# Attention and experts on one core: eight value products moved into the first five steps, the shared expert's preparation to the middle, the feed-forward weight splits to the end

## The reference, cut to what matters

```python
def _L0_attn_ref(X, Wq, bq, Wk, bk, Wv, bv, Wo, bo, gamma, beta, lam):   # B=2, S=1024, E=128, H=16, D=64
    Q = einsum('bse,hec->bhsc', X, Wq) + bq; K = einsum('bse,hec->bhsc', X, Wk) + bk    # c = 2D
    V = einsum('bse,hed->bhsd', X, Wv) + bv
    A1 = einsum('bhqd,bhkd->bhqk', Q[..., :d], K[..., :d]) / sqrt(d)
    A2 = einsum('bhqd,bhkd->bhqk', Q[..., d:], K[..., d:]) / sqrt(d)
    P = softmax(A1) - lam * softmax(A2)
    O = einsum('bhqk,bhkd->bhqd', P, V)
    Y = concat_heads(O) @ Wo + bo
    return layernorm(Y) * gamma + beta, times 0.2

def _L0_ffn_ref(x, alpha, w_gate, b_gate, W1m, b1m, W2m, b2m, W1e, b1e, W2e, b2e):
    main = gelu(x @ W1m + b1m) @ W2m + b2m                       # the shared expert, 128 -> 512 -> 128
    probs = softmax(mean(x, axis=1) @ w_gate + b_gate)           # 8 experts, top 2 of each batch
    expert_out = sum over the two of gate * (gelu(x @ W1e[k] + b1e[k]) @ W2e[k] + b2e[k])
    return a * main + (1 - a) * expert_out                       # a = clip(alpha, 0.1, 1)

xn = layernorm(x)
out = x + attn(xn) + ffn(xn)
```

## Time and profile before

| | |
|---|---|
| time, median of 3 runs (lowest to highest) | 1177.14 us (1176.85 to 1177.73) |
| the profiled execution's own time, and its span | 1176.92 us, 1175.1 us |
| PE, share of the span busy | 96% |
| POOL, ACT, DVE | 83%, 81%, 77% |

### The profile page before, as it was taken

How to read it: one execution, slowest core, us unless ns; L and a number is a source line. 1 busy time by engine, 2 the same in 40 slices (tenths; PEclk the granted TensorE clock), 3 DMA queues, 4 the chain that set the end, 5 groups by cost and what they waited for, 6 DMA issues and landing times.

```text
span 1175.1 us, 27816 instructions
## 1 busy us (share of the span) xinstructions
PE 1128.0 (96%) x9730; PEld 779.9 (66%) x9730; DVE 904.8 (77%) x1573; ACT 949.8 (81%) x1711; POOL 979.9 (83%) x609
## 2 busy tenths in 40 slices
PE   5899999999999999999999999999999999998998
PEld 4666666666666666666666666666666666664797
DVE  7878888888888888888888888888888888874510
ACT  3288899888898888898888898888898988885432
POOL 2589999999999999998888999999898888899000
PEclk9999999999999999999999999999999999998999
DMA  8942222222211222122212211222222212100000
GB/s 196 344 115 61 48 63 61 61 61 62 53 42 44 61 61 56 45 78 56 55 46 56 50 35 37 56 56 56 56 56 56 56 45 56 43 5 1 1 19 18
DMA packets 76439, 71.28 MB, mean 61 GB/s; under 512 B 43380, under 2 KB 65396, under 8 KB 76404
## 3 DMA queue, kind: packets, MB, share of 16 engines
q1 hardware_dynamic: 75396, 70.65, 23.1%
q10 hardware_dynamic: 880, 0.19, 0.1%
q0 software_dynamic: 128, 0.01, 0.0%
HBM read 22.59 MB, written 14.68 MB: 32 GB/s over the span
## 4 chain that ended last, share of the span: by engine, by line
PE 63%; ACT 20%; issue 6%; POOL 6%; DVE 4%; ACTq 1%; DMA 0%; DVEq 0%; SPq 0%; POOLq 0%
PE ps L567 20%; PE ps L535 18%; ACT work L753 11%; PE ps L553 10%; PE ps L489 8%; ACT p_mix L753 6%; POOL p_mix L448 3%; PE ps L652 3%; ACT pt L766 3%; PE ps L639 2%; POOL work L445 2%; PE ps L516 1%; DVE small L947 1%; DVE pt L903 1%; ACT small L719 0%
## 5 line engine op out<-in xcount | busy, mean ns | idle before, releaser
L947 DVE TENSOR_REDUCE small<-ps 128x1 f32<-128x1024 f32 x512 | 614.3, 1220 | 168.3 <-PE ps L535 168.3
L448 POOL TENSOR_TENSOR p_mix<-p_mix,work 128x1024 f32<-128x1024 f32 x256 | 608.8, 2378 | 21.4
L766 ACT ACTIVATE pt<-ps 128x512 f32<-128x512 f32 x512 | 306.8, 599 | 131.8 <-PE ps L553 129.7
L553 PE MATMUL ps<-ident,p_mix 64*128 64x64 f32 x4096 | 353.1, 227 | 5.6 <-POOL p_mix L448 2.8
L445 POOL TENSOR_SCALAR work<-work,small 128x1024 f32<-128x1024 f32 x256 | 307.4, 1201 | 50.4 <-DVE small L972 48.3
L553 PEld LDWEIGHTS ps<-ident,p_mix 64*128 64x128 f32 x4096 | 305.6, 139 | 55.9 <-issue 37.2
L753 ACT ACTIVATE p_mix<-ps,small 128x1024 f32<-128x1024 f32 x256 | 286.5, 1119 | 16.7 <-DVE small L947 16.7
L753 ACT ACTIVATE work<-ps,small 128x1024 f32<-128x1024 f32 x256 | 285.1, 1114 | 0.1
L567 PE MATMUL ps<-pt,v_h 128*64 128x512 f32 x1024 | 250.2, 610 | 0.7 <-ACT pt L766 0.7
L535 PE MATMUL ps<-k_hi,q_hi 64*128 64x512 f32 x512 | 227.5, 444 | 5.9 <-ACT p_mix L753 3.4
L535 PE MATMUL ps<-k_hi,q_lo 64*128 64x512 f32 x512 | 225.8, 441 | 0.0
(11 more groups left out here) (135 smaller groups left out, 1211.0 us busy)
## 6 DMA issues: line engine op xcount, KB each, us to landing
qx_hi<-q_hi SPq DMA_DIRECT2D x64, 256.0 KB, 3.8
qx_lo<-q_lo SPq DMA_DIRECT2D x64, 256.0 KB, 4.6
v_scratch<-pt SPq DMA_DIRECT2D x16, 512.0 KB, 5.4
v_h<-v_scratch SPq DMA_DIRECT2D x32, 256.0 KB, 3.1
w_scratch<-wqk_hi SPq DMA_DIRECT2D x16, 160.0 KB, 1.8
w_scratch<-wqk_lo SPq DMA_DIRECT2D x16, 160.0 KB, 1.9
wqk_hi<-w_scratch SPq DMA_DIRECT2D x16, 160.0 KB, 2.2
wqk_lo<-w_scratch SPq DMA_DIRECT2D x16, 160.0 KB, 2.3
```

What stands on the lines that cost most here:

```text
L448: pool.tensor_tensor(e1, e1, e2, ALU.add).then_inc(mix_done, 1)
L553: mm = pe.transpose(pt_ps[:, c * D:(c + 1) * D], p_mix[rows, col:col + P], ident[rows, rows])
L766: act.activation(pt4[:, kb % 2, :, j * P + half * D:j * P + (half + 1) * D], pt_ps.rearrange("p (c q) -> p c q", c=KC), ACT.Copy).then_inc ...
L947: dve.tensor_reduce(neg_max[:, m:m + 1], slot[SLOT[k, s]], AX.X, ALU.max, negate=True)\
```

## The change

**Values.** Parts 0 and 1 are computed before the second batch is transposed, parts 2 to 23 after it, and parts 24 to 31 inside steps 0 to 4 (two in each of the first three, one in each of the next two), behind the scores of the step. Parts 3, 7, 11, 15, 19 and 23 are copied out by ACT and get their bias from POOL, in SBUF. The other parts stay with DVE. SP stores tiles 0 to 11, then loads the values of head 0, then stores tiles 12 to 14, and tile 15 in its turn for head 1. POOL fills `y_acc` (`start_y`) after the weight split of head 1 in place of before it. In steps 0 to 7 the inverse sums come between the two row maxima.

**Experts.** The chosen experts' loads come after SP's work for head 2, and the preparation of the shared expert is spread over steps 119, 123, 127, 131, 135 and 139.

**First-layer weights.** The high parts are made by ACT, the low parts by DVE: one set after step 255, two after step 256 and two after step 257. The first hidden unit on PE comes one step earlier, and so does the first gelu on ACT.

```diff
-SET_MAIN = 5 + B
+SET_MAIN = 5 + 2 * B
+MAIN_AT, INPUT_AT = (119, 123), (127, 131, 135, 139)
...
+SPLIT_AT = {STEPS - 1: (0,), STEPS: (1, 2), STEPS + 1: (3, 4)}
+V_LATE = {0: (24, 25), 1: (26, 27), 2: (28, 29), 3: (30,), 4: (31,)}
+V_EARLY = 24
...
+        def by_act(u):
+            return u < V_EARLY and u % 4 == 3
+        def v_free(u):
+            return max([w for w in range(u) if v_place(w) == v_place(u)], default=None)
+        def v_out(u):
+            count = sum(by_act(w) == by_act(u) for w in range(u + 1))
+            return (v_copied if by_act(u) else v_evac), count
+        def v_place(u):
+            if u in (2, 3):
+                return u - 2
+            if u < V_EARLY + 2:
+                return 4 + (u + 2) % 4
+            return 6 if u in (26, 28) else 7
+        def v_part(u):
+            i, hv = divmod(u, 2)
+            return v_st[:, i % TB, hv * BANK:(hv + 1) * BANK]
...
-            for i in range(NT):
-                sp.wait_ge(v_evac, 2 * i + 2)
+            def store_v(i):
+                for u in (2 * i, 2 * i + 1):
+                    if by_act(u):
+                        sp.wait_ge(v_added, u // 4 + 1)
+                    else:
+                        sp.wait_ge(*v_out(u))
                 sp.dma_start(v_scratch[i, :, :], v_st[:, i % TB, :]).then_inc(v_stored[i % TB], 16)
+            for i in range(V_EARLY // 2):
+                store_v(i)
...
             for v in v_stored:
-                sp.wait_ge(v, 16 * B)
+                sp.wait_ge(v, 16)
             load_v(0, 0, 0)
+            for i in range(V_EARLY // 2, NT - 1):
+                store_v(i)
...
+                if n == 1:
+                    store_v(NT - 1)
...
+                if n == 2:
+                    load_experts()
+                if n == IT // B - 2:
+                    for v in v_stored:
+                        sp.wait_ge(v, 16 * B)
...
+                if n == MAIN_AT[1]:
+                    pool.tensor_scalar(w2[:, 0:HC * E], w2[:, 0:HC * E], coef[:, 0:1], one, ALU.mult, ALU.mult)\
+                        .then_inc(set_step, 1)
+                    pool.wait_ge(set_step, 3)
+                    pool.tensor_tensor(bias[:, 0, :], bias[:, 0, :], gb_bc[:, E:2 * E], ALU.add).then_inc(set_step, 1)
+                if n in INPUT_AT:
+                    part = INPUT_AT.index(n)
+                    pool.wait_ge(set_step, 5)
+                    add_row(bias[:, 0, :], part * TB // 2, (part + 1) * TB // 2)
...
-            start_y()
             for n in range(1, NW):
                 split_w(n)
-            set_main()
+            pool.wait_ge(xn_ready, 2 * B)
+            start_y()
+            def bias_v(first, end):
+                for u in range(first, end, 4):
+                    pool.wait_ge(*v_out(u))
+                    hv = u % 2
+                    pool.tensor_tensor(v_part(u), v_part(u), bv_bc[:, hv * BANK:(hv + 1) * BANK], ALU.add)\
+                        .then_inc(v_added, 1)
+            bias_v(3, V_EARLY)
...
-                s_ = k - TB - 1
-                if isinstance(g, int) and g == STEPS // BODY - 1 and 0 <= s_ < SETS:
-                    pool.wait_ge(s_ready, 2 * TB * (IT - 1))
-                    pool.tensor_scalar(w1_hi[s_], w1r3[:, s_, :], one, one, ALU.mult, ALU.mult)\
-                        .then_inc(w1_split, 1)
...
+            def values(u):
+                i, hv = divmod(u, 2)
+                if u in (2, 6):
+                    pe.wait_ge(lo_done, 1 if u == 2 else 2)
+                if u % 8 == 0:
+                    pe.wait_ge(xt_lo, i // 4 + 1)
+                if v_free(u) is not None:
+                    pe.wait_ge(*v_out(v_free(u)))
+                for j, (a, w) in enumerate(((xT_hi, wv_hi), (xT_lo, wv_hi), (xT_hi, wv_lo))):
+                    mm = pe.matmul(v_bank(u), a[:, i * P:(i + 1) * P],
+                                   w[:, hv * BANK:(hv + 1) * BANK], start=j == 0, stop=j == 2)
+                mm.then_inc(v_mm, 1)
+            pe.wait_ge(wv_split, 2)
+            values(0)
+            values(1)
             turn_x(1)
-
-
-            pe.wait_ge(wv_split, 2)
-            for i in range(NT):
-                for hv in range(2):
-                    u = 2 * i + hv
-                    bank = 4 + (u + 2) % 4
-                    if u == 2:
-                        pe.wait_ge(lo_done, 2)
-                    if u % 8 == 0:
-                        pe.wait_ge(xt_lo, i // 4 + 1)
-                    if u == 14:
-                        pe.wait_ge(route, 2)
-                        pe.wait_ge(small_loaded, 64)
-                        pe.matmul(ps[0:B, 2 * BANK:2 * BANK + NEXP], mean_tok, wg, start=True, stop=True)\
-                            .then_inc(route_mm, 1)
-                    after(pe, v_evac, u - 3)
-                    for j, (a, w) in enumerate(((xT_hi, wv_hi), (xT_lo, wv_hi), (xT_hi, wv_lo))):
-                        mm = pe.matmul(ps[:, bank * BANK:(bank + 1) * BANK], a[:, i * P:(i + 1) * P],
-                                       w[:, hv * BANK:(hv + 1) * BANK], start=j == 0, stop=j == 2)
-                    mm.then_inc(v_mm, 1)
-
-
-            pe.wait_ge(v_evac, 2 * NT)
+            for u in range(2, V_EARLY):
+                if u == 14:
+                    pe.wait_ge(route, 2)
+                    pe.wait_ge(small_loaded, 64)
+                    pe.matmul(ps[0:B, 2 * BANK:2 * BANK + NEXP], mean_tok, wg, start=True, stop=True)\
+                        .then_inc(route_mm, 1)
+                values(u)
...
+                if isinstance(g, int) and g == 0:
+                    for u in V_LATE.get(k, ()):
+                        values(u)
...
+                if c == 0:
+                    pe.wait_ge(w1_low, set_ + 1)
...
-                if k == 1:
+                if k == 0:
                     pe.wait_ge(exp_done, 2 * STEPS)
-                    pe.wait_ge(w1_split, 2 * SETS)
-                if 1 <= k <= OUT_LAG:
-                    hidden_mm(k - 1)
+                if k < OUT_LAG:
+                    hidden_mm(k)
...
+            def copy_v(u):
+                act.wait_ge(v_mm, u + 1)
+                after(act, v_stored[u // 2 % TB], 16 * (u // 2 // TB))
+                act.activation(v_part(u), v_bank(u), ACT.Copy).then_inc(v_copied, 1)
+            for u in range(3, 16, 4):
+                copy_v(u)
...
+            def high_w1(s_):
+                if s_ == 0:
+                    act.wait_ge(s_ready, 2 * TB * (IT - 1))
+                    act.wait_ge(main_loaded, 64)
+                    act.wait_ge(experts_loaded, 64 * (SETS - 1))
+                act.activation(w1_hi[s_], w1r3[:, s_, :], ACT.Copy).then_inc(w1_high, 1)
...
-                if k == 2:
+                if k == 1:
                     act.wait_ge(set_step, SET_STEPS)
-                if 2 <= k <= 4:
-                    gelu(k - 2)
+                if 1 <= k <= 3:
+                    gelu(k - 1)
...
+            def low_w1(s_):
+                dve.wait_ge(w1_high, s_ + 1)
+                dve.tensor_tensor(w1_lo[s_], w1r3[:, s_, :], w1_hi[s_].bitcast(F32), ALU.subtract).then_inc(w1_low, 1)
...
-                if j == 1 and now(g, k, 1):
+                soon = isinstance(g, int) and g == 0 and k < TB
+                if (j == 1 or soon and j != 3) and now(g, k, 1):
                     inv_sums()
                 p = k - 1
                 if p % TB in PROJ_AT and now(g, p, -TB):
...
                              slot[SLOT[p, "proj"]])
                 if now(g, k):
                     row_max(g, k, 1)
-                if j in (0, 2) and now(g, k, 1):
+                if j in (0, 2) and not soon and now(g, k, 1):
                     inv_sums()
+                if isinstance(g, int) and g == 0:
+                    for u in V_LATE.get(k, ()):
+                        evac_v(u, u + 1)
+                if isinstance(g, int) and (g * BODY + k - 1) in SPLIT_AT:
+                    for s_ in SPLIT_AT[g * BODY + k - 1]:
+                        low_w1(s_)
```

More of the change, by code:

```diff
@@ L542, in open_turn @@
                 if half == 0:
+                    if isinstance(g, int) and g * BODY + k == LAG:
+                        pe.wait_ge(*v_out(28))
                     pe.wait_ge(mix_done, n + 1)
@@ L560, in pv @@
                 if c0 == 0:
+                    if isinstance(blk, int) and blk == 0:
+                        pe.wait_ge(*v_out(2 * NT - 1))
                     pe.wait_ge(pt_evac, 2 * QB * (blk + 1))
@@ L588, in step @@
                         pe.wait_ge(q_crossed, 64 * (g * 2 + k // TB + 1))
+                    if isinstance(g, int) and (g, k) == (0, 1):
+                        pe.wait_ge(*v_out(V_EARLY - 2))
+                        pe.wait_ge(*v_out(V_EARLY - 1))
                     open_scores(g, k, 0)
@@ L724, in high_part @@
                 act.wait_ge(proj_mm, 2 * n + 1 + w)
+                if isinstance(n, int) and (n, w) == (1, 1):
+                    act.wait_ge(v_mm, 2 * NT)
                 if w == 0:
@@ L739, in _ @@
```

(7 more changed lines are left out.)

74 lines of the change are left out of this document (35 added, 39 removed).

## The result

The changed kernel takes 1169.07 us (median of 4 runs, 1167.64 to 1170.09), the kernel before 1176.99 beside it: 0.9934 of it, 95% interval 0.9922 to 0.9945, so 7.9 us or 0.7% faster. The forecast was 1172.1 with a range of 1167.0 to 1176.0. Six runs more, taken later, put the changed kernel at a median of 1168.25 over all ten. Its profiled execution took 1167.64 us with a span of 1165.7; that of before 1176.92 with 1175.1.

A forecast was written before the change was run, and what follows sets the result against it. The prediction took a PE chain with ACT copies to bound the middle, leaving only the two ends to win. Start -2.4, middle 0 and end -2.5 gave -4.9 on 1176.92: 1172.1 us, range 1167 to 1176.

The forecast's parts named there:

- first rival: Stores do not hold DVE, or the tail's extra waits are covered: about 1168.5 us, gain over 6.5; chance 0.22.
- Start, what gets earlier: Program start: DVE evacuations 1.1 us earlier, scores at 38.1 instead of 46.59, step 3's inverse sums 1.23 earlier in step 4.
- Start, what the stores give back: Program start: evacuations on DVE wait for value stores to land, leaving -2.4 us for the start, ends -0.8 and -5.
- the landing of tile 4: Value store in the start: issued at about 42.7, free at 46.9 us, so step 1's first maximum at 48.1, -2.8.
- Middle: nothing: Steps 119 to 139: POOL's waits hide the shared expert's six pieces, 0 us; uncovered they cost up to 7.4.
- End: Program end: last exponential 6.0 us earlier, stretch to the fifth hidden unit 23.5 instead of 19.7, so -2.5.
- gelu and table load ahead of block 255's copies: Tail: first gelu, table load and two splits, 3.6 us, delay PE's last transposes; half is covered, 1.8 us counted.
- the first hidden unit behind the low part: Tail: first hidden unit waits for DVE's low part, which gets in only when POOL's instruction ends: 0.8 us.
- The granted clock left out: Whole program: no term for the granted clock in the sum, since waits of PE both go and come.
- The walk at the end: From step 254's start at 1062.86 to the last exponential's end at 1073.9 us, against 1079.91: -6.0.
- The second (waits take all): Rival: slow landings (-0.8) and the low part behind a whole mix (0) leave -0.8, 1176 us; chance 0.16.
- The third (the pieces not hidden): Rival: the shared expert's pieces make PE wait, 7.4 us come back, 1179.4 us; chance 0.10 with other losses.

The follow-up runs named there:

- the halves: Kernel before with only the changed start and middle: 1171.94 us, ratio 0.9953; kernel before with only the changed end: 1174.55 us, ratio 0.9980.

## Why the forecast came out as it did

The direction and the range held. The gain was 7.9 and not 4.9, in the band of the first rival (over 6.5) without its mechanism: stores do hold DVE, as the three landing waits show. Step by step:

**Start, what gets earlier.** The row of 128x8 fell from 1.32 to 0.17 as forecast, and rose again to 1.32 when the fill went back. Both rows agree with the Trainium skill (SBUF — State Buffer, Who interferes with whom), by which a DVE instruction with two SBUF inputs contends with a POOL instruction that reads SBUF. But the forecast had this 1.1 us at the front of everything, and in the new order 0.3 of it was left behind the stores. The scores came at 38.86 (38.1 forecast). The earlier inverse sums gave 0.6 to 1.2 (1.23).

**Start, what the stores give back.** The chain of events was right: tile 3 free at 41.5 (42.0), first maximum 42.16 (42.6). What failed is a size, the landing of tile 4. The sum took 42.7 plus 4.2, 46.9, where the median of the earlier trace rows is 3.8. It was issued at 42.06 and DVE went on at 44.92, 2.9 later, near the fastest of the earlier trace rows. The forecast named that case, -4.8 for the first maximum of step 1, and did not take it; it was -4.75. Steps 1 to 3 then took 8.0 (8.5), so step 3 stood at -4.0 and not at -1.6. This is 2.4 of the 3.3 us by which the start was under-sized (-5.7 by step 10 against -2.4). The rest lies behind step 3: POOL's fourth mix came 6.2 earlier, where the forecast had 2.8. Some 1.1 of this went with the half-level stretch at 60 to 64 us of before, as with the fill moved alone. And the expert's preparation, 7.4 us long, would have cost 2.1 in the new start. The forecast asked what moving it costs in the middle, and never what it would cost where it stood once the scores come 8 us sooner.

**Middle: nothing.** Right. The lead is 5.77 at step 10 and 5.6 at step 204, the exponentials' starts compared. POOL's waits between 500 and 640 us shrank from 10.0 to 4.1, so the pieces lie in them, and no new wait of PE appeared there.

**End.** The last exponential was forecast 6.0 earlier by the end's part and was 6.5 (12.1 less 5.6). The give-back was forecast at 3.8 and was 2.8: gelu and table load ahead of block 255's copies 1.8 (measured 1.72), second output product 0.8 (0.80), copies behind splits 0.4 (0.3, the remainder), the first hidden unit behind the low part 0.8 (0: DVE waited 0.24 for the high part, PE not at all). So -3.7 by the traces. The last of these was the mis-sized one: a POOL instruction beside it did grow, from 1.20 to 1.73, but DVE's did not.

**The granted clock left out.** The forecast put it at nothing, "since waits of PE both go and come here", and that is the other step that failed, as a term put at nothing. The walk at the end took full-clock durations (1.94 for eight value products) against a kernel that ran them at half (the row below), so 1.7 of its 6.0 was clock without saying so. With the clock held equal by the fit the halves are worth 3.2 and 0.9, together 4.1. That this is close to the 4.9 is partly chance, as the forecast had 2.4 and 2.5 for them. By the same reading of runs, the measured 8 contain 4 more that go with a clock that no term described.

The eight value products ahead of block 253's transposes, before and after:

```profile
1073.67 3.68 PE L567 MATMUL ps<-pt,v_h 128*64 128x512 f32 x8
```

```profile
1063.48 2.06 PE L633 MATMUL ps<-pt,v_h 128*64 128x512 f32 x8
```

**Rivals and signs.** The second (waits take all) fell with the fast landings. The third (the pieces not hidden) fell with POOL's waits in the middle. Of the signs, DVE's waits for landings, PE's wait of 1.72 and scores at 38.86 came as named; step 1's first maximum, 4.75 us earlier and not 2 to 3, and the last exponential, at 1066.70 and not at 1069 to 1071, already said that the start was worth more than its term.

## What to carry to other kernels

When work is moved away from a place, price it where it would stand after the rest of the change, not where it stands now: the forecast let the expert's preparation cost nothing at its old place, and in the new start it would have cost 2.1 us. A helper engine that takes over part of a copy but leaves a second pass to a third engine can cost more than it spares, when a store waits for both. When two executions are subtracted, look whether both had the same granted clock: where a wait of PE goes, a slow stretch behind it may be gone as well, and the difference then holds both.

## What had not been expected of the hardware

Runs of one program differ in time chiefly as their mean granted clock does, 0.63 us for 0.001: the kernel before lay at 1174.7 to 1177.0 at 0.994 and 0.995 and at 1182.6 and more at 0.984. One place shows the same: with 1.1 us taken from DVE at 17 us, and PE's wait at 19 us down from 2.46 to 0.69, the fourth mix came 2.7 earlier, and two stretches at 1.2 GHz were gone from that execution. And of 2x8 and 128x8 instructions of DVE three took 1.2 to 1.3 us instead of 0.2, each beside a POOL instruction, while DVE's 128x512 evacuations beside POOL's additions kept their 0.6 to 0.7.
